# Second expert layer of a two-layer vision transformer: the sorted token blocks in chunks of 10, 10 and 8 instead of 8, 12 and 8

## The reference, cut to what matters

```
logits = xf @ router_weight.T ; scores = sigmoid(logits) ; s_choice = scores + router_bias
# 16 experts in 4 groups of 4; the 2 groups with the highest sum of their top 2 stay; top 4 experts of those
w = scores of the 4 ; w = w / (sum(w) + 1e-20) * 2.5
for e in range(16):  out += combine[:, e:e+1] * ((silu(xf @ w_gate[e].T) * (xf @ w_up[e].T)) @ w_down[e].T)
h = h + out          # xf is the layer norm of h
```

## Time and profile before

| what | value |
|---|---|
| three timed executions | 1642.79, 1649.74 and 1649.97 us (median 1649.74) |
| the profiled execution | 1643.09 us, its span 1641.3 us |
| mean granted clock of PE | 0.924 |
| busy share of the span: PE, DVE, ACT, POOL | 85%, 64%, 46%, 40% |
| second expert layer | from about 1196 us to the end of the span |

### The profile page before, as it was taken

The page is one execution under the profiler, slowest core; times in us unless marked ns, Lnnn a source line. Parts: engine busy times, 40 slices in busy tenths (PEclk is TensorE's granted clock), DMA queues, the critical chain, the costliest instruction groups (busy, mean ns, idle before and its releaser), DMA issues. The chain is left out here.

```text
span 1641.3 us, 37317 instructions
## 1 busy us (share of the span) xinstructions
PE 1390.6 (85%) x14157; PEld 1222.5 (74%) x14188; DVE 1049.6 (64%) x2196; ACT 757.0 (46%) x1288; POOL 661.7 (40%) x888
## 2 busy tenths in 40 slices
PE   6979999999999976688962788899767899889882
PEld 5867888888888866688862576667567889889882
DVE  4654575476476477765665468888758766466654
ACT  5324444444444433254541566677522365556520
POOL 4015312112111005466264354333365666663665
PEclk9989999999999997899995899999857999999997
DMA  7305655325325005247651010000082377877843
GB/s 278 116 27 169 224 168 190 105 87 190 111 91 172 2 5 215 78 148 238 207 174 37 14 33 8 1 2 2 2 307 71 113 254 236 259 232 232 240 126 90
DMA packets 142885, 215.59 MB, mean 131 GB/s; under 512 B 14336, under 2 KB 112768, under 8 KB 141824
## 3 DMA queue, kind: packets, MB, share of 16 engines
q1 hardware_dynamic: 121648, 160.20, 29.5%
q0 software_dynamic: 18624, 52.45, 10.2%
q10 hardware_dynamic: 2448, 0.61, 0.2%
HBM read 103.64 MB, written 109.58 MB: 130 GB/s over the span
## 5 line engine op out<-in xcount | busy, mean ns | idle before, releaser
L125 PE MATMUL e_p_gu<-e_w_hi,e_xt_hi 128*128 (+1 forms) x676 | 202.0, 299 | 12.2 <-DVE e_xt_lo L724 8.6
L125 PE MATMUL e_p_gu<-e_w_lo,e_xt_hi 128*128 (+1 forms) x676 | 196.0, 290 | 0.0
L125 PE MATMUL e_p_gu<-e_w_hi,e_xt_lo 128*128 (+1 forms) x676 | 196.0, 290 | 0.0
L1275 POOL DMA_INDIRECT e_xn<-results,e_row_of x112 | 114.3, 1020 | 77.3 <-issue 47.9
L125 PEld LDWEIGHTS e_p_gu<-e_w_hi,e_xt_hi 128*128 128x128 f32 x676 | 134.1, 198 | 14.4 <-issue 12.4
L125 PEld LDWEIGHTS e_p_gu<-e_w_lo,e_xt_hi 128*128 128x128 f32 x676 | 134.7, 199 | 0.0
L125 PEld LDWEIGHTS e_p_gu<-e_w_hi,e_xt_lo 128*128 128x128 f32 x676 | 134.4, 199 | 0.0
L125 PE MATMUL e_p_y<-e_w_hi,e_hid_hi 128*128 (+1 forms) x338 | 113.3, 335 | 8.4 <-DVE e_hid_lo L743 7.1
L1256 POOL DMA_INDIRECT rows<-e_xn,e_row_of x96 | 94.8, 988 | 54.2 <-issue 47.2
L125 PE MATMUL a_J<-a_xt_hi,w_qk_hi 128*128 128x512 f32 x256 | 106.7, 417 | 7.4 <-DVE a_xt_lo L1960 5.4
L1942 DVE TENSOR_TENSOR a_ot_lo<-a_O,a_ot_hi 128x1024 fp32r<-128x1024 f32 x32 | 39.1, 1223 | 114.5 <-ACT a_ot_hi L1885 114.5
(11 more groups left out here) (335 smaller groups left out, 4393.9 us busy)
## 6 DMA issues: line engine op xcount, KB each, us to landing
e_moved<-rows SPq DMA_DIRECT2D x121, 256.0 KB
results<-e_y SPq DMA_DIRECT2D x121, 256.0 KB
rows<-a_zero SPq DMA_DIRECT2D x28, 1024.0 KB, 5.8
pa_x<-in_x SPq DMA_DIRECT2D x7, 1536.0 KB, 6.3
w_qk_in<-in_we SPq DMA_DIRECT2D x24, 384.0 KB, 6.3
we_parts<-w_qk_in SPq DMA_DIRECT2D x24, 384.0 KB, 2.5
we_parts<-a_e_lo SPq DMA_DIRECT2D x24, 384.0 KB, 2.4
e_w_hi<-we_parts SPq DMA_DIRECT2D x4, 1536.0 KB, 16.1
```

Source lines behind the costliest of these rows:

```text
L125: mm = eng.matmul(out, lhs[a], rhs[b], start=start and n == 0, stop=stop and n == len(terms) - 1, skip_group_check=skip)
L1275: pool.indirect_dma_start(out=yg[g % RING][:, k, :], out_offset=None, in_=d["results"][c][0:rooms[c] * P], in_offset=bass.IndirectOffsetOn ...
```

## The change: what it does

```diff
-CHUNKS = ((0, 8), (8, 20), (24, 32))
+CHUNKS = ((0, 10), (10, 20), (24, 32))
```

## The result

| | median us | runs | lowest to highest | ratio to before |
|---|---|---|---|---|
| before | 1646.15 | 16 | 1640.29 to 1650.44 | |
| after | 1656.37 | 16 | 1651.93 to 1660.66 | 1.0064 [1.0049, 1.0078] |

The change costs 10.2 us, 0.64% with an interval of 0.49% to 0.78%: slower, by a little more than the 0.5% that the prediction named as the edge. The forecast was 1655 (1644 to 1665), +8.3 us on the profiled execution.

A forecast was written before the change was run, and what follows sets the result against it. POOL's queue was taken to bound the end: +16.7 at step 51, -2.6 `row_of` slack, -3.1 gather 0 and vanished wait, -2.7 gather 2, giving +8.3 us, 1651.4 on the profiled execution. Written as 1655 us, range 1644 to 1665.

The forecast's parts named there:

- The eight scatters are on the path to PE's first pair: Chunk 0's eight added scatters, 13.3 us, are covered by nothing; PE starts chunk 0's pairs 17.1 us later.
- the later start: Chunk 0's scatter on POOL starts later: one router step, 2.48 us, plus 1.3 us for routing 10 blocks.
- PE's restart: PE after its wait for chunk 0's first load: costs what it did, at 1.2 GHz some 6 us; 1 us either way.
- From there to `row_of` of chunk 2: PE's first pair to step 51: 0.4 us off for lighter routing pieces of chunk 1, leaving everything 16.7 us later.
- step 51: Step where chunk 2's `row_of` is ready, before and after; predicted 16.7 us later, bounds 14.5 to 18.5.
- POOL's two new waits: POOL waits some 14 us for `row_of` before chunk 2's scatter and some 11 us before gather 2.
- Chunk 1's scatter: Eight scatters less, both chunks together still 80; POOL's 3.12 us wait goes and POOL is done at 1372, as before.
- Gather 0: POOL's gathers of chunk 0: 40 transfers, 67.5 us, starting 14.1 us later, at 1439.3.
- The level of 1655: Forecast time: 1651.4 us on the profiled execution, 1654.7 on the middle of four executions, 1646.4; written as 1655.
- POOL would not wait before gather 2: Rival, not slower: gather 2 follows gather 1's 40 gathers at once, 2.8 us earlier, about 1640.3 us; chance 0.12.
- POOL never waits: Rival, faster: POOL runs through from 1372.1, gather 2 16.9 us earlier, 1626 us; chance 0.06.
- the scatters slow down: Rival: eight transfers at 1467 instead of 972 ns add 4.0 us, +12.3 in all, 1655.4 us; chance 0.12.

The follow-up runs named there:

- the experiment that took this wait away: Kernel after with chunk 1's combines moved to steps 94 to 114, off the last pair of chunk 2; 1645.52 us.
- all three edits: Kernel after with chunk 2's routing at two pieces a step, chunk 0's combines from step 71 and chunk 1's at 94 to 114; 1635.90 us.
- the experiments that made gather 0 early: Kernel after with chunk 2's routing at two pieces a step: 1658.05 and 1656.52 us alone; 1643.17, 1647.42 and 1635.90 us with combines moved too.
- the routing edit: Kernel after with chunk 2's routing at two pieces a step instead of one, run twice; 1658.05 and 1656.52 us.

## Why the prediction was right

**The eight scatters are on the path to PE's first pair: right.** +4.0 us for the later start (3.8 forecast) and +17.1 us at PE (17.1 forecast). That the second fits to the tenth is luck: chunk 0's last scatter (1286.62 before, 1309.46 after) began 17.4 us later counted from the start of the layer, and PE's first pair then followed it 5.5 us later, in place of 5.9. Leaving the eight out took 12.5 us off PE's wait, where 13.3 were costed. PE's restart was as assumed: in the 6 us around the end of a wait of 17.96 us the granted clock was 0.50, the 1.2 GHz level, as in the earlier trace rows after 3.75 us.

```profile
1314.00:1320.00 6.00, 5.00 (x23) 4.54 (x24) 2.70 (x4) 1.45 (x3) 3.78 (x7) 0.50 0.86 302
```

**From there to `row_of` of chunk 2: the term that was mis-sized.** I took 0.4 us off for lighter routing pieces; measured, the way from PE's first pair to `row_of` took 77.2 us instead of 76.0, +1.2. So step 51 came 18.2 us later and not 16.7, inside the bounds of 14.5 to 18.5. Busy times and clock over this way (columns as above), the whole of it before and after:

```profile
1292.54:1368.54 76.00, 70.46 (x566) 67.94 (x567) 53.70 (x155) 41.64 (x90) 50.38 (x91) 0.96 0.68 219
```

```profile
1315.00:1392.17 77.17, 72.43 (x566) 69.83 (x567) 53.30 (x155) 42.48 (x91) 41.91 (x76) 0.94 0.65 208
```

DVE's work did fall by 0.4 us, 53.70 to 53.30. But PE was busy 2.0 us longer with the same number of products, at a lower granted clock. In the kernel after the clock fell a second time, some 27 us after the restart and for 3.4 us; before, it stayed at full speed from the restart to `row_of`. The 8 us ahead of the fall and the fall itself, then the same 8 us of the kernel before, counted from PE's first pair, and the whole way behind its restart:

```profile
1333.00:1341.00 8.00, 5.71 (x47) 5.13 (x45) 4.93 (x14) 2.93 (x7) 5.42 (x10) 1.00 0.91 312
1341.60:1345.00 3.40, 3.40 (x18) 3.40 (x17) 1.24 (x4) 0.86 (x2) 2.16 (x4) 0.50 0.51 177
```

```profile
1310.54:1318.54 8.00, 5.42 (x44) 4.85 (x43) 4.66 (x14) 2.81 (x7) 5.46 (x11) 1.00 1.00 319
1298.54:1368.54 70.00, 64.80 (x542) 62.87 (x541) 50.87 (x151) 40.19 (x87) 46.36 (x84) 1.00 0.69 218
```

At half clock, 3.4 us of work lose 1.7 us by an estimate from these rows; with the 0.4 us less that makes +1.3, close to the +1.2 measured. The other traces go the same way. In the three with the chunks of before this way took 75.7, 76.0 and 77.0 us, each at a mean clock of 0.96; in the three with those of after and the routing in single pieces 77.2, 78.3 and 80.4 us, at 0.94, 0.92 and 0.91. So the price that I had at nothing is PE's clock behind the restart; no run here set the clock by itself, so this is argued from the traces. Why the clock fell again is open: PE was a little less busy in the same 8 us of the kernel before, and it did not fall there. The error goes through to the end.

**POOL's two new waits: right in place and size.** 15.43 us before chunk 2's scatter (14 forecast) and 11.76 us before gather 2 (11 forecast). Chunk 1's scatter had next to no net effect, as costed: POOL was through with both chunks at 1377.76 (1393.19 - 15.43), so with the usual 0.78 us it could have begun chunk 2's scatter 176.6 us from the start of the layer, against 175.6 before. Gather 0 took 68.4 us instead of 67.5, and gather 2 followed gather 1 by 79.2 instead of 79.9. The sum of these three errors is +1.5, +0.9 and -0.7, which is the 1.7 us by which gather 2 missed, and but for 0.1 us the end.

**The level of 1655.** The sum gave 1651.4 us on the profiled execution, which is below the lowest of the 16 runs after, 1651.93. The step to 1655 took the middle of four executions, 1646.4, for the kernel before; 16 runs put it at 1646.15. That four executions from 1642.79 to 1649.97 gave it so well was luck.

**The rivals.** That POOL would not wait before gather 2 fell by the trace, and the experiment that took this wait away gave its case: 0.6 us under before on the medians, where it was priced at 2.8 under. That POOL never waits fell too; its closest form, all three edits, came to 1635.90, 10.6 us under the kernel before where it was priced at 16.9, since a wait of 5.31 us stays. That the scatters slow down fell by their spacing in chunk 0, 1.666 us after ((1309.46 - 1244.47) / 39) against 1.664 before, and by their durations, in ns:

```profile
L1256 POOL DMA_INDIRECT rows<-e_xn,e_row_of x96: 968/971/1358, 1271.8 to 1444.1; - x96
```

Their median is 971 against 972, and the longest of these 96 is shorter; among the first 16 scatters, which are listed apart, the longest took 1617 ns (1353 before). The rule of the Trainium skill, page "SBUF — State Buffer", section "Who interferes with whom", that of two instructions of VectorE and GpSimd that want the shared port pair one is fully blocked, would show as longer scatters where it is the scatter that waits. The median shows no such lengthening; why single scatters took up to 1617 ns is not shown.

**What the prediction did not see.** The ring of three gather buffers is tied to the step of the first combine, and had 5 us of slack. It did not bear on this change, since gather 0 came late enough; it decided the experiments that made gather 0 early. That the ring holds POOL there is shown by the releaser of the wait and by its fall from 12.19 and 15.02 to 4.92 us, and to none with all three edits, when the first combine moved four steps ahead. Why one execution of that kernel lost PE's clock in those steps and the other did not stays open.

## What to carry to other kernels

On an engine whose queue runs in order, list what ties each stage of it (an input that is ready at a fixed step, a buffer that comes free, results that must be stored) with the slack of each: a stage that starts later or gets shorter turns the slack of the next tie into a wait, and one wait taken away is won only up to the next smallest slack. A transfer that moved ahead of the first work of a chunk was paid there in full, even though the total count stayed (12.5 us for eight), and its delay came back at the steps that are tied to that work. Work that another engine does at a fixed step, such as these combines, should stand where its data have arrived: moving it by a few steps gave 8.8 us on the kernel before and 10.9 us on the one after, about as much as the change cost.

## What the runs showed that was not expected

The same program does not reach the second expert layer at the same time: the two executions of the routing edit began it at 1206.37 and 1201.53 us, and over all the kernels here it began between 1196.28 and 1206.37. In the three executions with the chunks of before it began between 1196.50 and 1197.70, in the eight with those of after the spread is wider; whether the change has a part in that is not shown. Counted from this start, the difference of two profiled executions came close to that of the medians in some cases (10.1 and 10.2 us for the change, 19.8 and 20.5 for all three edits) and not in others (8.8 and 13.9 for the eight scatters).

PE's granted clock can differ between two executions of one kernel in the same steps: in the stretch from 130 to 170 us after the start of the layer it was 1.00 in one execution of the routing edit, and 0.83 and then 0.91 in the other. Such falls go with the differences of the way to chunk 2's `row_of` between traces, 75.7 to 80.4 us.
